# Copying the first 32 pair results out of the bank on VectorE instead of ScalarE

## The reference

```python
xn = layernorm(x)
# branch 1: a recurrence with 16 states, gated
u = xnn @ Ws.T + bs + xnn @ Wi.T + bi          # xnn = layernorm(xn) * ln_w + ln_b
h_t = tanh(h_{t-1} @ A.T + u_t)                # over the 2048 steps
s = (H @ Wo.T + bo) * sigmoid(xnn @ Wg.T + bg) + xn
# branch 2: 16 experts, the best 4 of each token, and one shared expert
c = 2.5 * normalised sigmoid scores of the 4 chosen experts
y = sum_e c[:, e] * ((silu(gate_e) * up_e) @ w2[e].T)  + shared expert
out = x + s * silu(y)
```

## Time and profile before

| | |
|---|---|
| runs, us | 515.88, 516.11, 516.85 |
| profiled execution, us | 515.73 |
| its span, us | 513.9 |
| mean granted TensorE clock, share of full | 0.837 |
| TensorE busy, us | 339.1 (66%) |
| VectorE busy, us | 311.1 (61%) |
| ScalarE busy, us | 251.0 (49%) |
| GpSimd busy, us | 265.4 (52%) |

### The profile page before, as it was taken

How to read it: one execution, slowest core, us unless ns; L and a number is a source line. 1 busy time by engine, 2 the same in 40 slices (tenths; PEclk the granted TensorE clock), 3 DMA queues, 4 the chain that set the end, 5 groups by cost and what they waited for, 6 DMA issues and landing times.

```text
span 513.9 us, 10001 instructions
## 1 busy us (share of the span) xinstructions
PE 339.1 (66%) x3107; PEld 261.7 (51%) x3107; DVE 311.1 (61%) x977; ACT 251.0 (49%) x462; POOL 265.4 (52%) x278
## 2 busy tenths in 40 slices
PE   0365566849467786976799968797876968645210
PEld 0352443626355665755698846575654756433100
DVE  4899776676703545545643626786776555346745
ACT  1851666536434455443787746565664644422000
POOL 2005377766646566655600165766555554436773
PEclk9976698797876889888999989999997898676555
DMA  7998499425443566654779768899977777436653
GB/s 247 305 328 281 129 343 331 161 86 201 143 165 127 175 186 201 196 172 156 216 220 269 227 192 268 281 282 285 285 243 211 249 217 225 128 119 194 174 160 126
DMA packets 88675, 109.27 MB, mean 213 GB/s; under 512 B 9649, under 2 KB 78002, under 8 KB 88626
## 3 DMA queue, kind: packets, MB, share of 16 engines
q1 hardware_dynamic: 74656, 74.47, 45.7%
q0 software_dynamic: 12288, 33.57, 20.7%
q10 hardware_dynamic: 1682, 0.59, 0.4%
HBM read 55.91 MB, written 52.69 MB: 211 GB/s over the span
## 4 chain that ended last, share of the span: by engine, by line
PE 35%; another core or an unknown queue 12%; issue 10%; ACT 8%; DVE 6%; POOL 5%; DMA 1%; ACTq 1%; POOLq 0%; DVEq 0%
PE bank L850 13%; PE bank L872 8%; PE bank L656 6%; POOL xn_parts L638 5%; PE bank L863 3%; ACT xn_f L1851 3%; PE bank L898 2%; ACT sh_h L1868 1%; ACT y_ring L1875 1%; ACT xn_f L1859 1%; ACT x_ring L1881 1%; PE bank L948 1%; DVE mix_sb L1371 1%; PE bank L774 1%
## 5 line engine op out<-in xcount | busy, mean ns | idle before, releaser
L638 POOL DMA_INDIRECT xn_parts<-y_slots,slot_u x128 | 127.2, 994 | 126.2 <-PE bank L656 39.6
L619 POOL DMA_INDIRECT x_slots<-xn_parts,slot_u x128 | 131.7, 1029 | 115.1 <-DVE slot_u L1253 36.0
L850 PE MATMUL bank<-w_all,xn_f 128*128 (+1 forms) x864 | 122.2, 295 | 22.2 <-issue 11.5
L850 PEld LDWEIGHTS bank<-w_all,xn_f 128*128 128x128 f16 x864 | 87.3, 106 | 44.8 <-issue 30.6
L1524 DVE SCALAR_TENSOR_TENSOR xn_f<-bank,xn_f 128x256 f32<-128x256 f32 x72 | 30.5, 424 | 111.9 <-ACT xn_f L1859 69.3
L1851 ACT ACTIVATE xn_f<-bank 128x1024 f16<-128x1024 f16 x72 | 73.5, 1022 | 36.7 <-remote 22.3
L872 PE MATMUL bank<-w_all,sh_silu 128*128 (+1 forms) x432 | 68.2, 299 | 5.5 <-ACT y_ring L1875 4.2
L1875 ACT ACTIVATE y_ring<-bank 128x512 f32<-128x512 f32 x72 | 42.9, 596 | 54.4 <-PE bank L872 33.7
L1859 ACT ACTIVATE xn_f<-bank 128x256 f32<-128x256 f32 x72 | 27.5, 382 | 55.0 <-remote 32.4
L656 PE MATMUL bank<-ident_h,w_stage 128*128 128x128 f16 x576 | 48.6, 231 | 1.5 <-issue 1.4
L872 PEld LDWEIGHTS bank<-w_all,sh_silu 128*128 128x128 f16 x432 | 41.8, 106 | 14.5 <-issue 7.5
(11 more groups left out here) (215 smaller groups left out, 456.9 us busy)
## 6 DMA issues: line engine op xcount, KB each, us to landing
w_stage<-x_slots SPq DMA_DIRECT2D x72, 256.0 KB
y_slots<-y_ring SPq DMA_DIRECT2D x72, 256.0 KB
x_slots<-zero_h SPq DMA_DIRECT2D x10, 1024.0 KB
x_ring<-in_x SPq DMA_DIRECT2D x32, 256.0 KB
w_stage<-in_w13t SPq DMA_DIRECT2D x17, 256.0 KB
x_ring<-in_x SPq DMA_DIRECT2D x8, 512.0 KB, 7.7
out<-mix_sb SPq DMA_DIRECT2D x15, 256.0 KB
w_stage<-in_w2t SPq DMA_DIRECT2D x17, 128.0 KB
```

What stands on the lines that cost most here:

```text
L619: eng.indirect_dma_start(out=x_slots, out_offset=bass.IndirectOffsetOnAxis(ap=slot_u[:, n * TOPK + k:n * TOPK + k + 1], axis=0), in_=xn_pa ...
L638: eng.indirect_dma_start(out=fin_y[:, r, j, k, :], out_offset=None, in_=y_slots[0:2 * READY_PAIR[c] * P, :], in_offset=bass.IndirectOffset ...
L850: mm = eng.matmul(gu[:, j * 2 * F:(j + 1) * 2 * F], xg_T[:, n % 2, ((j * 2 + px) * KD + k) * P:((j * 2 + px) * KD + k + 1) * P], weights_o ...
```

## The change

`pair_y_out` is written a second time, for VectorE, with `tensor_copy` and the same two waits. VectorE's pass n calls it at its very end, behind slot 3n+2, for n from 2 to 33, so for the results of pairs 0 to 31. ScalarE's loop calls its own only from pass 34 on, for pairs 32 to 71. Nothing else is changed: TensorE, SyncE and GpSimd have the instructions they had.

```diff
@@ -91,6 +91,7 @@
     VL = 8
+    Y_VECTOR = 32
@@ -1538,6 +1539,12 @@
+            def pair_y_out(n):
+                eng.wait_ge(pair_down, n + 1)
+                if n >= YS_RING:
+                    eng.wait_ge(y_out[n % YS_RING], y_landed(n - YS_RING))
+                eng.tensor_copy(y_ring[:, n % YS_RING, :, :].rearrange("p b d -> p (b d)"), YP[:, :]).then_inc(pair_y, 1)
+
@@ -1687,6 +1694,8 @@
                 if 1 <= n <= NPAIR:
                     pair_h(n - 1)
                 beside(SLOTS * n + 2)
+                if 2 <= n < Y_VECTOR + 2:
+                    pair_y_out(n - 2)
@@ -1920,7 +1929,7 @@
                 beside(SLOTS * n + 1)
                 beside(SLOTS * n + 2)
-                if n >= 2:
+                if n >= Y_VECTOR + 2:
                     pair_y_out(n - 2)
```

## The result

The changed kernel took 522.61 us (median of five runs, 520.16 to 523.64), five runs of the kernel before beside it 516.11 us (514.05 to 516.85). The ratio is 1.0105, with a 95% interval from 1.0068 to 1.0142: some 5.4 us slower, between 3.5 and 7.3; the two medians lie 6.5 us apart. The forecast was 519.7 us with a range up to 522.2; the sign is right and the size too small. In the profiled execution the time is 523.53 us, the span 521.7 us and the mean clock 0.838.

The account below looks back on a forecast made before the run. TensorE was taken to bound passes from 252 to 292 us, the recurrence those before. Terms of 0.8 + 1.3 + 1.5 = 3.6 us on 516.11 gave 519.7 us, range 514.4 to 522.2.

Parts of the forecast that it names:

- the sign: Whole kernel: the change makes it slower, chance 0.60 (0.50 for the forecast, 0.10 for a falling clock).
- What bounds the kernel: TensorE without idle time from 252 to 292 us; before that the recurrence through three engines; delays reach the end.
- The relief of ScalarE: 32 copies of 0.596 us leave ScalarE; a rival had this count and VectorE's queue not: 513.2 us, chance 0.18.
- The price of a copy: One f32 copy on VectorE lasts 0.68 us, taking 0.60 us of its queue, against 0.596 on ScalarE.
- Term 1: Passes 3 and 8: the recurrence's sum starts 0.6 us later each; pass 13 gains 0.4; together 0.8 us lost.
- Term 2: Pass 20: pair 18's copy waits behind route_weights on VectorE, and TensorE stands still for 1.3 us.
- Term 3: Passes 31 and 33: copies of pairs 29 and 31 wait behind mixing; TensorE slips 0.75 us each, 1.5 us.
- the passage on the plain passes: Passes without special work: the copy lands 0.7 us later with 0.4 us left; store and load slip, costing nothing.
- The clock rival: A halt of 1.3 us in pass 21 lowers the clock, costing two more microseconds: 521.7 us; chance 0.10.
- The sum: Six special passes: 0.8 + 1.3 + 1.5 = 3.6 us slower in all.

Follow-up runs that it names:

- copy ahead: Changed kernel with VectorE's copy moved ahead of route_weights in pass 20 and of out_mix in passes 31 and 33; 524.27 us, 1.0014 of the kernel before.

## Why the prediction was right, and where not

- **What bounds the kernel**: right. The even stage is TensorE's; its 2.63 us stayed, no step between pairs 24 and 36 was given back, and of the 7.07 us at pair 36 6.5 were there at the last store. The relief of ScalarE gained nothing that shows (pairs 0 to 15: 1.0013, from 0.9983).
- **The price of a copy**: right, 0.683 us for 0.68. The Trainium skill, "VectorE: DVE Perf Modes", The perf-mode tier table, has twice the basic rate as the most for a copy with an operand in PSUM, and this f32 one doesn't reach it; the section Why PSUM operands drop a tier has the basic rate for fp32, and the trace agrees: 0.683 us, as much as L1552 with its two f32 operands (0.680).
- **Term 1** (0.6 + 0.6 - 0.4): the mechanism is there in its place, by the medians from the cast +0.5, +0.5 and -0.4. That it reaches the time is not shown: a few passes on the products are where they were within the scatter, and pairs 1 and 6 alone measured 0.9978 (up to 1.0004), not the 1.0023 that 1.2 us would give. Passes of the recurrence differ by up to 2 us between profiles of kernels that are alike there.
- **Term 2** (1.3): 1.14 alone, 1.48 in the whole change.
- **Term 3** (1.5): 0.79 + 0.90 alone. In the profile of the changed kernel pass 31 paid only 0.19 of it, since TensorE was late already.
- **The step that failed** is in the passage on the plain passes: "SyncE's store goes out as much later, and so does the load queued behind it; that load is used three passes on, so it costs nothing." It looked at the rows of the next pairs only. Behind the store of pair 25 `place_states` stands in the same queue, with a user that already waited 0.20 us. Charged with nothing, it took 3.0 us of the passes from pair 31 to 33: 0.63 later issue and a slower landing made a wait of 1.27, and the low clock behind it cost 1.66.
- **The clock rival**: the mechanism was real and its price about right (1.66 us, with 2 forecast), but it struck elsewhere. In pass 21 TensorE stood 1.48 us and the next twelve L851 took 1.47, at full clock; it was pass 31 where the clock fell.
- **The sum**: 3.6 us were forecast. The terms as read in the changed kernel's profile give, with term 1 as forecast, 0.8 + 1.4 + 3.0 (pairs 31 to 33) + 1.3 (pairs 33 to 36) = 6.5, and the ratio of the runs 5.4; without term 1, which no time shows, it is 5.7. With the states at nothing and the late copies of pairs 29 and 31 at the 1.9 that they cost alone, the sum would have been 4.1, near the forecast. That 3.6 came within 2 us of the 5.4 is in part luck: term 1 may be nothing, and pass 31's copy hid behind the late states, so two errors made up for a part of the one that counted. The median stood 0.4 us above the top of the range.

**What stays open.** The steps of a repair and its ratio don't agree to better than a microsecond, so the share of each term in the total is known less well than its place. The states also landed more slowly in some kernels: 6.8 to 7.0 us from the issue to `out_mix` in the changed kernel, its repeat, "copy ahead", but also with pair 11 alone (276.53 to 283.44), where the issue was not late; it waited 0.74 us and has a step of 1.00 from 31 to 32, the exception named above. Of the wait of 1.27 us, then, 0.20 was there before, 0.63 belongs to the queue by every profile, and the rest may be scatter. Why the landing differs wasn't tried. Nor was the halt of several us that every kernel has soon after its first gathers; its size differed between profiles by 1 to 2 us, enough to blur the offsets from pair 37 on.

## What to carry to other kernels

When an operation moves to another in-order queue, price it twice: for what it waits behind there, and for everything that is queued behind whoever waits for it, rare work too. List every DMA behind a store that now starts later, over the whole stretch, and look for the user with the least slack; one pass of the loop does not show it. A copy out of a bank that the next matmul must overwrite belongs ahead of side work in its queue, not at the end: the same 32 copies cost 0.7 to 1% at the end, and nothing that could be measured once three of them stood ahead and one load came early.

## What the runs showed of the hardware

- The same f32 copy of 128x512 out of a bank takes 0.683 us on VectorE and 0.597 on ScalarE; 16-bit results of the same number of elements take VectorE 0.417.
- Idle stretches of TensorE of 1.27 us and 0.48 behind it were followed by a granted clock of 0.50 in pass 31, and so were 1.26 and 0.75 in the repeat and 1.46 and 0.75 in "copy ahead"; 0.83 and 0.47 (pairs 19 to 28) were not, nor 0.74 and 0.75 (pair 11 alone), nor a single one of 1.48 in pass 21 or of 2.14 with pairs 29 and 31 alone. What tells these apart wasn't settled.
- Three DMAs issued in a row took SyncE 1.35 us before and 2.58, 2.20, 2.13 and 2.18 in the four kernels where pair 25 was on VectorE and the states stood in slot 86; in all others 1.35 to 1.38. Nothing in these instructions differs.
